# Smaller, deeper batches in the third layer of a four-layer graph network

## The reference

```
e_w   = sigmoid(silu(edge_attr @ edge_W1 + b1) @ edge_W2 + b2)     # one weight per edge
x_agg = silu(x[src] @ agg_W + agg_b) * e_w
out   = segment_sum(x_agg, dst) / max(count, 1)
h     = silu(concat(x, out) @ upd_W1 + upd_b1) @ upd_W2 + upd_b2 + x @ res_W
```

## Time and profile before

| | |
|---|---|
| median of 3 runs | 1179.43 us (1178.74 to 1180.83) |
| the profiled execution | 1179.85 us, its span 1178.0 us |
| third layer's gathers and scatters in the profile | 756.1 to 1020.6 us |
| PE matmul busy over the span | 1033.8 us, 88% |
| DVE busy over the span | 1014.4 us, 86% |
| ACT (ScalarE) busy over the span | 463.6 us, 39% |

### The profile page before, as it was taken

One profiled execution on the slowest core, in us unless ns is written; L12 is line 12 of the kernel. 1 busy time (PEld: TensorE's weight loads), 2 busy tenths in 40 slices (PEclk: granted clock), 3 DMA queues, 4 the chain that ended last, 5 costly groups with the idle time before them and its releaser, 6 DMA issues.

```text
span 1178.0 us, 27820 instructions
## 1 busy us (share of the span) xinstructions
PE 1033.8 (88%) x10937; PEld 902.0 (77%) x10937; DVE 1014.4 (86%) x2121; ACT 463.6 (39%) x1103; POOL 86.3 (7%) x124
## 2 busy tenths in 40 slices
PE   4897978899999999919999997799999999917994
PEld 3343566799999999906777777599999999816784
DVE  6767999999999999899888997889989889796445
ACT  3566846122222222158888896400000000154663
POOL 4404040000000000030000000000000000030000
PEclk9898999899999999958999998899999999958997
DMA  5000020544444444104333342122222222123882
GB/s 147 1 1 2 3 63 7 175 147 147 147 147 149 150 169 146 32 1 168 117 118 118 107 122 70 47 86 80 82 88 76 87 88 75 68 71 108 253 228 55
DMA packets 70757, 116.21 MB, mean 99 GB/s; under 512 B 8443, under 2 KB 47302, under 8 KB 70396
## 3 DMA queue, kind: packets, MB, share of 16 engines
q1 hardware_dynamic: 70201, 113.56, 30.7%
q10 hardware_dynamic: 426, 0.85, 0.3%
HBM read 91.14 MB, written 23.24 MB: 97 GB/s over the span
## 4 chain that ended last, share of the span: by engine, by line
PE 76%; DVE 14%; ACT 4%; DMA 2%; issue 2%; POOL 0%; POOLq 0%; DVEq 0%; SPq 0%; ACTq 0%
PE PS L1901 14%; PE PS L2085 13%; PE PS L1889 10%; PE PS L2073 9%; PE PS L2124 6%; PE PS L2006 6%; PE PS L1974 3%; PE PS L1981 3%; PE PS L1727 2%; PE PS L1740 2%; ACT X L1002 2%; DVE st L1473 2%; DVE vo L1284 1%; DMA adj_d<-ring 1%; DVE ring L1280 1%
## 5 line engine op out<-in xcount | busy, mean ns | idle before, releaser
L1263 DVE TENSOR_TENSOR vo<-iotam,SLr 128x768 f32<-128x768 f32 (+1 forms) x218 | 212.2, 974 | 30.9 <-PE PS L2085 27.1
L1901 PE MATMUL PS<-vo 128*128 128x133 f32 x1300 | 175.9, 284 | 1.4 <-DVE vo L1357 1.4
L2085 PE MATMUL PS<-vo 128*128 128x128 f32 x1300 | 169.7, 280 | 2.9 <-DVE vo L1621 2.9
L1901 PEld LDWEIGHTS PS<-vo 128*128 128x128 f32 x1300 | 157.2, 191 | 1.5 <-issue 1.5
L2085 PEld LDWEIGHTS PS<-vo 128*128 128x128 f32 x1300 | 154.8, 193 | 3.1 <-DVE vo L1263 3.1
L1889 PE MATMUL PS<-kp,ring 128*128 128x132 bf16 x1950 | 146.2, 220 | 3.6 <-DVE ring L1256 2.1
L1889 PEld LDWEIGHTS PS<-kp,ring 128*128 128x128 bf16 x1950 | 125.3, 97 | 5.8 <-DVE ring L1256 2.2
L2073 PE MATMUL PS<-kp,ring 128*128 128x128 bf16 x1950 | 126.5, 219 | 0.8 <-ACT big L1064 0.8
L979 ACT ACTIVATE vo<-lz,negc 128x24 f32<-128x24 f32 (+1 forms) x109 | 34.6, 318 | 230.1 <-DVE lz L1348 230.1
L1046 ACT CAST ring<-PS 128x512 bf16<-128x512 f32 (+1 forms) x175 | 119.6, 693 | 9.4 <-DMA adj_d<-ring 9.4
L1043 ACT CAST adjf_r<-PS 128x512 fp32r<-128x512 f32 (+1 forms) x175 | 118.7, 686 | 6.5 <-PE PS L1974 5.6
(11 more groups left out here) (316 smaller groups left out, 1833.5 us busy)
## 6 DMA issues: line engine op xcount, KB each, us to landing
ring<-rows_d SPq DMA_DIRECT2D x146, 416.0 KB, 3.9
adj_d<-ring SPq DMA_DIRECT2D x100, 128.0 KB, 1.7
adj_d<-ring SPq DMA_DIRECT2D x75, 96.0 KB, 1.8
ring<-adj_d SPq DMA_DIRECT2D x11, 640.0 KB, 4.2
vo<-adj_d SPq DMA_DIRECT2D x9, 640.0 KB, 5.3
vo<-adj_d SPq DMA_DIRECT2D x8, 480.0 KB, 4.8
ring<-adj_d SPq DMA_DIRECT2D x7, 480.0 KB, 4.7
big<-rows_d SPq DMA_DIRECT2D x4, 416.0 KB, 5.9
```

Source lines behind the costliest of these rows:

```text
L1263: V.tensor_tensor(ohd[:, k % 3, 0:n, :], iotam[:, :].unsqueeze(1).to_broadcast([P, n, P]), SLr[:, 1, t[0]:t[-1] + 1].unsqueeze(2).to_broad ...
L1901: T.matmul(bank(6 + b % 2)[:, 0:VW], ohd[:, k % 3, i, :], vals[:, k % 3, i, :], start=j == 0, stop=j == JN - 1).then_inc(scattered, 1)
L2085: T.matmul(bank(6 + q % 2)[:, (b % 4) * P:(b % 4 + 1) * P], vals[:, k % 3, i, 0:F], ohd[:, k % 3, i, :], start=j == 0, stop=j == JN - 1).t ...
```

## The change

In the third layer alone the batch becomes four tiles (BT2 = 4), which makes 163 batches, the last one of two tiles. A batch's gathered values take one PSUM bank, four tiles at 128 columns each, and there are four sets (VB2 = 4), in banks 0 to 3; `vals2` and `ohd2` have four sets too. PE gathers three batches ahead of the scatter, in place of two, so that it starts with gathers of batches 0, 1 and 2 and goes on with gather k+3, scatter k. The gather of batch k waits for the values of batch k-4. On DVE the one-hot of destinations of batch k waits for the scatter of batch k-4, the source one-hots of a unit are built six batches ahead of the batch that needs them first, and the sums of a quad are taken out four batches after its last one. The first layer is not touched.

```diff
--- before.py
+++ after.py
@@ -21,6 +21,8 @@
 VW = ROW0 + 1
 GW = 160
 BT = 6
+BT2 = 4
+VB2 = 4
 ATT = 96
 ATK = ATT + 3
 ATW = ATK + 1
@@ -119,6 +121,11 @@
     def batch(k):
         return range(BT * k, min(BT * k + BT, NT))
 
+    def batch2(k):
+        return range(BT2 * k, min(BT2 * k + BT2, NT))
+
+    NBATCH2 = -(-NT // BT2)
+
     def source(t):
         return t % JN if t % JN < NB else t // JN
 
@@ -226,6 +233,8 @@
         vo = sb("vo", [P, 3 * BT * (VW + P)])
         vals = vo[:, 0:3 * BT * VW].rearrange("p (r t k) -> p r t k", r=3, t=BT)
         ohd = vo[:, 3 * BT * VW:3 * BT * (VW + P)].rearrange("p (r t k) -> p r t k", r=3, t=BT)
+        vals2 = vo[:, 0:VB2 * BT2 * F].rearrange("p (r t k) -> p r t k", r=VB2, t=BT2)
+        ohd2 = vo[:, 3 * BT * VW:3 * BT * VW + VB2 * BT2 * P].rearrange("p (r t k) -> p r t k", r=VB2, t=BT2)
         adj3v = vo[:, 0:3 * ACH * 2 * P].bitcast(bf16).rearrange("p (r k n) -> p r k n", r=3, k=ACH)
         PAY = vo[:, 0:PAYS * JN * CW].bitcast(bf16).rearrange("p (r c k j) -> p r c k j", r=2, k=PAYS, j=JN)
         g_row = vo[:, 0:ROW0]
@@ -542,6 +551,9 @@
         def batch_end(k):
             return min(BT * (k + 1), NT)
 
+        def batch_end2(k):
+            return min(BT2 * (k + 1), NT)
+
         def on_act(s):
             return s % 2 == 0
 
@@ -1602,28 +1614,39 @@
                     dve.wait_ge(rc_out, 32)
                 V.tensor_tensor(AG[:, cols(q)], bank(6 + q % 2)[:, 0:width(q)], rcB[:, cols(q)], ALU.mult).then_inc(ag_ready, 1)
 
-            def sums_at(k):
-                return [q for q in range(BANKS) if k == (JN * (blocks(q)[-1] + 1) - 1) // BT + 3]
-
-            for h in units_at(0):
+            def sums_at(q):
+                return (JN * (blocks(q)[-1] + 1) - 1) // BT2 + 4
+
+            def units_at2(k):
+                return [h for h in range(NU) if max(0, (HT * h) // BT2 - 6) == k]
+
+            def dst_hots2(k):
+                t = batch2(k)
+                n = len(t)
+                if k >= VB2:
+                    dve.wait_ge(scattered, NT + batch_end2(k - VB2))
+                V.tensor_tensor(ohd2[:, k % VB2, 0:n, :], iotam[:, :].unsqueeze(1).to_broadcast([P, n, P]),
+                                SLr[:, 1, t[0]:t[-1] + 1].unsqueeze(2).to_broadcast([P, n, P]), ALU.is_equal).then_inc(hots_dst, 1)
+
+            for h in units_at2(0):
                 edge_hots(h, 0, 1)
-            dst_hots(0, 1)
-            for k in range(NBATCH):
-                n = len(batch(k))
-                a = -(-n // 3)
+            dst_hots2(0)
+            for k in range(NBATCH2):
+                t = batch2(k)
+                n = len(t)
                 if k:
-                    for h in units_at(k):
+                    for h in units_at2(k):
                         edge_hots(h, 0, 1)
-                if k + 1 < NBATCH:
-                    dst_hots(k + 1, 1)
-                dve.wait_ge(gathered_up, NT + batch_end(k))
-                t = batch(k)
-                V.tensor_tensor(vals[:, k % 3, 0:n, 0:F].rearrange("p (a i) f -> p a i f", a=a), gathered(k, 0, F),
-                                EWS[:, t[0]:t[-1] + 1].rearrange("p (a i) -> p a i", a=a).unsqueeze(3).to_broadcast([P, a, n // a, F]), ALU.mult).then_inc(vals_ready, 1)
-                for q in sums_at(k):
-                    sums_out2(q)
+                if k + 1 < NBATCH2:
+                    dst_hots2(k + 1)
+                dve.wait_ge(gathered_up, NT + batch_end2(k))
+                V.tensor_tensor(vals2[:, k % VB2, 0:n, :], bank(k % VB2)[:, 0:n * F].rearrange("p (i f) -> p i f", f=F),
+                                EWS[:, t[0]:t[-1] + 1].unsqueeze(2).to_broadcast([P, n, F]), ALU.mult).then_inc(vals_ready, 1)
+                for q in range(BANKS):
+                    if sums_at(q) == k:
+                        sums_out2(q)
             for q in range(BANKS):
-                if (JN * (blocks(q)[-1] + 1) - 1) // BT + 3 >= NBATCH:
+                if sums_at(q) >= NBATCH2:
                     sums_out2(q)
             with dve.If(general == 1):
                 sums(2)
@@ -2063,12 +2086,12 @@
             pe.wait_ge(xp_mid, BANKS)
 
             def gather2(k):
-                if k >= 3:
-                    pe.wait_ge(vals_ready, NBATCH + k - 2)
-                for i, t in enumerate(batch(k)):
+                if k >= VB2:
+                    pe.wait_ge(vals_ready, NBATCH + k - VB2 + 1)
+                for i, t in enumerate(batch2(k)):
                     h, l = t // HT, t % HT
                     pe.wait_ge(hots_src, 2 * NU + h + 1)
-                    to = spot(k, i)
+                    to = 512 * (k % VB2) + i * F
                     for part in range(3):
                         o = T.matmul(PS[:, to:to + F], ohT[:, 0, h % OBUF, l * P:(l + 1) * P], XP[:, source(t), part, :],
                                      start=part == 0, stop=part == 2)
@@ -2077,19 +2100,19 @@
             def scatter2(k):
                 pe.wait_ge(hots_dst, NBATCH + k + 1)
                 pe.wait_ge(vals_ready, NBATCH + k + 1)
-                for i, t in enumerate(batch(k)):
+                for i, t in enumerate(batch2(k)):
                     b, j = t // JN, t % JN
                     q = b // 4
                     if j == 0 and b % 4 == 0 and q >= 2:
                         pe.wait_ge(ag_ready, 1 * BANKS + q - 1)
-                    T.matmul(bank(6 + q % 2)[:, (b % 4) * P:(b % 4 + 1) * P], vals[:, k % 3, i, 0:F], ohd[:, k % 3, i, :],
+                    T.matmul(bank(6 + q % 2)[:, (b % 4) * P:(b % 4 + 1) * P], vals2[:, k % VB2, i, :], ohd2[:, k % VB2, i, :],
                              start=j == 0, stop=j == JN - 1).then_inc(scattered, 1)
 
-            gather2(0)
-            gather2(1)
-            for k in range(NBATCH):
-                if k + 2 < NBATCH:
-                    gather2(k + 2)
+            for k in range(VB2 - 1):
+                gather2(k)
+            for k in range(NBATCH2):
+                if k + VB2 - 1 < NBATCH2:
+                    gather2(k + VB2 - 1)
                 scatter2(k)
             with pe.If(general == 1):
                 sums(2)
```

## The result

The changed kernel took 1184.68 us in the median (1182.25 to 1185.62, 7 runs), the kernel before 1180.21 beside it. The ratio is 1.0037, with a 95% interval of 1.0025 to 1.005, or +4.4 us (+3.0 to +5.9). In a second measurement it was 1184.47 us, ratio 1.0043 (1.0028 to 1.0058), or +5.1 us. The forecast had the right sign, but +2.4 us, 1181.8 us, and a range that ended at 1184.0. Of the 2.9 us by which the median lies above the forecast, 0.8 is the kernel before itself, at 1180.21 beside the 1179.43 from which the forecast was added up; the other 2 are growth that the forecast did not have.

What follows compares the result with a forecast made beforehand. PE's instruction stream was taken to bound the third layer. Gather-to-scatter changes +2.65, start -0.80 + 0.34 + 0.17, end 0: +2.36 on 1179.43 gave 1181.8 us, own range 1181.0 to 1182.6, outer ends 1179.6 and 1184.0.

Steps and rivals of the forecast that it cites:

- What bounds the stage: Third layer: as long as PE's instruction stream; PE busy 258.37 of 258.40 us, waiting for DVE only once.
- The turns: Third layer on PE: each change from gather to scatter costs 0.050 us; 53 more of them add 2.65 us.
- rival 2: Third layer, first matmul of every scatter: changing from gather to scatter costs nothing; 1179.1 us; chance 0.08.
- DVE under PE: Third layer: DVE's 1.39 us per batch stays under PE's 1.615, 0.22 us of room, hiding 108 more operations.
- Rival 3: Third layer: DVE becomes the bound, its batch exceeding PE's; +1.6 to +4.9 us on top, 1183.4 to 1186.7; chance 0.08.
- The start: Third layer's first scatter: values 0.80 us earlier, +0.34 for gathers left over, +0.17 for slow clock; sum -0.29 us.
- rival 1: Third layer's first scatter: the clock stays at 2.4 GHz, taking back 1.71 us; +0.65, 1180.1 us; chance 0.17.
- the end: Behind the third layer's last gather: 28 scatter matmuls in both kernels, dense update waits for the last as before; 0 us.
- rival 4: Stages behind the third layer: a later stage meets the slow clock otherwise, 1.6 us either way, 1180.2 or 1183.4; chance 0.12.
- The sign of being wrong that the prediction names last: Third layer's batch period is right, yet the total moves by more than 1 us beyond the forecast.

Runs made afterwards that it cites:

- bare delay: Kernel before, one tile's three gather matmuls of third-layer batch 54 issued 14 times more, a 2.35 us delay: 1183.96 us, ratio 1.0043.

## Why the prediction missed

**What bounds the stage** was right: PE is busy for 261.68 of 261.70 us after, and waits for nothing but the first scatter.

**The turns** were right, and rival 2, by which they cost nothing, did not come. 0.050 us each was read from the earlier trace rows; the period came to 1.617 us for a forecast of 1.615, and doubling and halving the turns moved the stage the way they should (+7.2 and -4.2 us, for +5.3 and -3.9).

**DVE under PE** was right: 683 to 696 ns for its operations of 512, 24.5 us of waiting for PE, and no wait of PE for it in the steady part. Rival 3 did not come. I had read the section "The DRAIN you can't avoid" of the Trainium skill's "VectorE: DVE Perf Modes" as a rule that the trace contradicts; the section itself says that a next operation that is not held starts earlier, so the overlapping starts of the earlier trace rows need be no disagreement with it.

**The start** was right: first gather to first scatter 0.87 us shorter (forecast 0.80), in the second profile 1.0; the clock fell there as before, so rival 1 did not come.

**The step that failed is the end**, put as "the dense update waits for the last of them as before: 0", with nothing for all that follows the stage. It measured +2.1 to +2.2 us. The shift of everything behind the stage had two effects in the last layer, both of them the clock. The larger, 1.5 us: it moved the pause of TensorE against the clock's changes, the stretch with most of the pause held 1.44 us of TensorE's work in place of 1.92, and the 3.4 us behind it were granted 1.2 GHz. The smaller, 0.4 us: 48 matmuls lay a little deeper in the slow stretch that was there before, the one of the earlier trace rows. The remaining 0.2 us are open. The bare delay shows that the shift is enough for both, and the addition cut into seven shows that the larger needs the pause.

It is rival 4 on the slower side, which I had given a chance of 0.12, for both sides together, at 1.6 us. The stretch that I named for it is the place of the smaller effect and not of the larger. I took its sign for a matter of luck, "either way", and that was the second mistake: in two profiles of each kernel the fall was there or not in the same way. In these profiles the first gather of the third layer lies at almost the same distance behind an earlier fall of the clock near 506 us: 250.2 and 250.0 us before, 250.3 and 250.2 after, and between 250.0 and 250.5 in 12 of all 14. Why the clock keeps step with the program so well is not known. From the trace of before I could have laid the pause of 1077.4 to 1079.9 us beside the end of the slow stretch at 1069.1. That would have named this pause as a place that a shift endangers; whether the clock would fall there, no row of before says.

The sign of being wrong that the prediction names last did come: the period was right, and the total moved by 2.0 us beyond the forecast. That the median also left the range is partly chance: the same growth on the 1179.43 us of the forecast would be 1183.8, inside 1184.0.

The stage and the last part together grew by 4.6 us in the first pair of profiles and by 4.5 in the second, for a measured 4.4 and 5.1 between the times. The opening is left over: 1.2 us later in the profile of after, but in the other profiles its first gather lies anywhere from 754.4 to 757.8 us, and the bare delay reaches the same ratio without it. Still, five of the six profiles with the smaller batches have it at 757.3 or later, and none of the eight without them after 757.0. Whether the changed program also makes the opening longer is open.

## What to carry to other kernels

Where TensorE bounds a stage, count how often it changes from one kind of matmul to the other, here from bf16 gathers to fp32 scatters. Smaller batches buy such changes, and alternating in longer groups sells them back without touching any other engine. And before pricing a delay at its own length, look at each later pause of TensorE and at each slow stretch: a shift of 2 us cost 4 here. A pause taken away gained the wait and, where the clock had fallen behind it, the slow clock too.

## What the runs showed of the hardware

- A turn from the bf16 gathers to the fp32 scatters, each matmul with its own weights, costs 0.05 us at 2.4 GHz, with batches of 3, 4, 6 and 8 tiles (half a period of 1.23 us and periods of 1.617, 2.398 and 3.18), with or without a wait in front. The turn back showed no cost: 12 and 18 gathers behind a scatter take 0.67 and 1.00 us, 0.056 us each. I had taken the Trainium skill ("TensorE: Matmul & The Clock Gate", "Part 2: What happens when you issue a matmul") as the rival that a load is hidden behind the running matmul. In these traces 0.05 us per turn are left; whether they are a part of a load that is not hidden, no run shows.
- Nearly the same place of the work against the clock's changes came back in profile after profile, so that a loss to the clock looked like a property of the program. In the four profiles in which the clock fell behind the pause, the 32 matmuls there took 9.16 to 9.24 us; in the seven others that have the pause, 7.66.
